# Segment sums of a graph kernel: gathered rows as the stationary operand, three tiles at a time

## The reference

```python
# part 1: two relational layers (8 relation types), then a layer norm
h = x
for l in range(2):
    W = einsum('rb,bio->rio', coeff[l], basis[l])
    msg = einsum('ni,rio->rno', h, W)[etype, src] * norm
    h = segment_sum(msg, dst, 2500) + bias[l]
    if l < 1: h = relu(h)
x = layernorm(x + h)
# part 2: three mean-aggregation layers, then a layer norm
h = x @ W_in + b_in
for l in range(3):
    agg = segment_sum(h[src], dst, 2500) / max(degree, 1)
    h = relu(agg @ W_agg[l] + h @ W_self[l] + b_hid[l])
out = layernorm(x + h @ W_out + b_out)
```

## Time and profile before

| | us |
|---|---|
| median of 3 runs (2393.61 to 2397.88) | 2394.03 |
| the profiled execution, its own time | 2401.69 |
| its span in the profile | 2399.9 |
| PE busy, matmuls | 1803.5 (75%) |
| POOL busy | 1255.5 (52%) |
| DVE busy | 1197.4 (50%) |
| ACT busy | 625.7 (26%) |

### The profile page before, as it was taken

The page is one execution under the profiler, slowest core; times in us unless marked ns, Lnnn a source line. Parts: engine busy times, 40 slices in busy tenths (PEclk is TensorE's granted clock), DMA queues, the critical chain, the costliest instruction groups (busy, mean ns, idle before and its releaser), DMA issues.

```text
span 2399.9 us, 29813 instructions
## 1 busy us (share of the span) xinstructions
PE 1803.5 (75%) x7695; PEld 1342.2 (56%) x7695; DVE 1197.4 (50%) x3965; ACT 625.7 (26%) x1520; POOL 1255.5 (52%) x1294
## 2 busy tenths in 40 slices
PE   4667677677677676757677777776666679999997
PEld 2455455455455454535455555555555567777776
DVE  5747654544445445335555555553268743232355
ACT  1112222222222222212222322222111124633332
POOL 5766666666666666366666666666666630000000
PEclk9879888988889899879989888899888789999998
DMA  6333333333333333233333333334533320000011
GB/s 209 93 89 97 99 98 98 100 97 98 99 99 97 99 99 99 59 92 101 102 100 98 105 99 100 103 101 122 169 102 96 98 61 11 1 1 1 1 35 44
DMA packets 118622, 208.19 MB, mean 87 GB/s; under 512 B 53828, under 2 KB 74196, under 8 KB 118456
## 3 DMA queue, kind: packets, MB, share of 16 engines
q0 software_dynamic: 62016, 169.04, 24.8%
q1 hardware_dynamic: 48848, 26.08, 3.8%
q10 hardware_dynamic: 7592, 11.13, 1.4%
HBM read 189.01 MB, written 17.13 MB: 86 GB/s over the span
## 4 chain that ended last, share of the span: by engine, by line
PE 50%; another core or an unknown queue 17%; issue 14%; DVE 13%; ACT 3%; DVEq 2%; DMA 1%; ACTq 0%; POOL 0%
PE bank L662 15%; PE bank L828 11%; PE bank L615 8%; DVE RY L455 4%; PE bank L650 4%; DVE RY L444 2%; PE bank L593 2%; PE bank L845 2%; PE bank L773 2%; DVE RY L379 1%; DVE RY L378 1%; DMA RX<-in_basis 1%; ACT RY L560 1%; DVE rdeg L390 1%
## 5 line engine op out<-in xcount | busy, mean ns | idle before, releaser
L662 PE MATMUL bank<-RY 128*128 128x256 f32 x2580 | 864.3, 432 | 11.6 <-issue 4.6
L250 POOL DMA_INDIRECT RY<-H,si x645 | 619.4, 960 | 367.0 <-issue 152.4
L250 POOL DMA_INDIRECT RY<-in_x,si x645 | 635.8, 986 | 333.1 <-issue 147.5
L444 DVE TENSOR_TENSOR RY<-RY,bank 128x256 f32 x430 | 180.8, 420 | 900.7 <-remote 694.8
L662 PEld LDWEIGHTS bank<-RY 128*128 128x128 f32 x2580 | 487.1, 220 | 109.4 <-issue 42.0
L650 PE MATMUL bank<-idn,RY 128*128 128x128 f32 x860 | 193.4, 311 | 394.7 <-issue 245.9
L455 DVE TENSOR_SCALAR RY<-iot,c,wgt 128x128 f32<-128x128 f32 x1290 | 461.8, 370 | 1.5 <-issue 1.5
L560 ACT COPY RY<-bank 128x256 f32<-128x256 f32 x430 | 161.1, 375 | 973.2 <-PE bank L662 519.8
L650 PEld LDWEIGHTS bank<-idn,RY 128*128 128x128 f32 x860 | 116.5, 158 | 503.4 <-issue 451.0
L828 PE MATMUL bank<-Ar,hs 125*128 125x500 f32 x1200 | 305.8, 405 | 0.0
L828 PEld LDWEIGHTS bank<-Ar,hs 125*128 125x128 f32 x1200 | 225.7, 188 | 51.7 <-issue 9.2
(11 more groups left out here) (106 smaller groups left out, 1163.2 us busy)
## 6 DMA issues: line engine op xcount, KB each, us to landing
RY<-in_x,si POOLq DMA_INDIRECT x645
RY<-H,si POOLq DMA_INDIRECT x645
Ad<-RY SPq DMA_DIRECT2D x215, 40.0 KB
RX<-Ad ACTq DMA_DIRECT2D x20, 305.2 KB
RX<-in_basis ACTq DMA_DIRECT2D x2, 2048.0 KB, 34.3
H<-RY SPq DMA_DIRECT2D x22, 128.0 KB
RY<-in_x SPq DMA_DIRECT2D x22, 128.0 KB
X<-RY SPq DMA_DIRECT2D x22, 128.0 KB
```

What stands on the lines that cost most here:

```text
L250: e.indirect_dma_start(G[0:k, n % NG, :], None, table, bass.IndirectOffsetOnAxis(ap=si[0:k, t:t + 1], axis=0)).then_inc(s_land[n % NG], 16)
L444: e.tensor_tensor(o, o, bank[4 + wg % 2][:, 0:256].rearrange("p (q c) -> p q c", c=16), ALU.add).then_inc(s_za, 1)
L662: e.matmul(bank[2 + wg % 2][:, 0:256], S[0:k, n % NSL, :], G[0:k, n % NG, :], start=(i == 0), stop=(i == TA - 1)).then_inc(s_sum, 1)
```

## The change

The sums are produced with features on the partitions at once. For each group, at its last tile, PE issues six matmuls: for each half of the features (c = 0, 1) and each of the three tiles, the half of the gathered rows `G` (128x128) is the stationary operand and `S` (128x128) the moving one. Both halves of a group lie in one bank, and the groups take banks 2 to 5 in turn. DVE adds that bank to `ZA` directly. The copy to `Zs`, the transposes and their semaphores are gone. `s_sum` still counts tiles, now each at its matmul for c = 1, the last reader of its slots. The waits elsewhere that named the removed semaphores name `s_sum`, `s_za` or `s_win`; the region `RY` is laid out without `Zs`.

```diff
@@ -172,9 +172,9 @@
 
         with ExitStack() as inner:
             RY = inner.enter_context(nc.sbuf_tensor("RY", [128, 20480], F32))
-        (Mr, Nr, Aw, Aw8, E2, G, S, Zs, W2, ZA, Ew, Pg, hw, h1w, xw, xT) = lay(
+        (Mr, Nr, Aw, Aw8, E2, G, S, W2, ZA, Ew, Pg, hw, h1w, xw, xT) = lay(
             RY, ((NSL, 128), BF16), ((NSL, NB), BF16), ((4, NB), BF16), ((4, NB), U8), ((2, 128), BF16), ((NG, 256), F32),
-            ((NSL, 128), F32), ((2, 256), F32), ((2, 2048), F32), ((2, 16 * ZC), F32), ((2, 128), F32), ((2, 256), F32),
+            ((NSL, 128), F32), ((2, 2048), F32), ((2, 16 * ZC), F32), ((2, 128), F32), ((2, 256), F32),
             ((2, 256), F32), ((2, 256), F32), ((2, 256), F32), ((2, 256), F32))
         ZA = ZA.rearrange("p s (q c) -> p s q c", c=ZC)
         diag = [v[:, k, h * 128:(h + 1) * 128] for v in (xw, xT) for k in range(2) for h in range(2)]
@@ -198,7 +198,7 @@
         s_land = [sem(f"s_land{i}") for i in range(NG)]
         s_sel, s_sum = sem("s_sel"), sem("s_sum")
 
-        s_zs, s_turn, s_za = sem("s_zs"), sem("s_turn"), sem("s_za")
+        s_za = sem("s_za")
 
         s_clear, s_carry1, s_prod, s_pg = sem("s_clear"), sem("s_carry1"), sem("s_prod"), sem("s_pg")
         s_hw, s_h1w, s_h1 = sem("s_hw"), sem("s_h1w"), sem("s_h1")
@@ -440,8 +440,8 @@
                 e.wait_ge(s_clear, 4 * (l * NW + g + 1))
             else:
                 e.wait_ge(s_za, wg)
-            e.wait_ge(s_turn, wg + 1)
-            e.tensor_tensor(o, o, bank[4 + wg % 2][:, 0:256].rearrange("p (q c) -> p q c", c=16), ALU.add).then_inc(s_za, 1)
+            e.wait_ge(s_sum, l * T + min(T, TA * w + TA))
+            e.tensor_tensor(o, o, bank[2 + wg % 4][:, 0:256].rearrange("p (q c) -> p q c", c=16), ALU.add).then_inc(s_za, 1)
 
         def dve_layer(e, l):
             for t in range(T + (TAIL if l == 0 else 2)):
@@ -552,12 +552,6 @@
                         act_clear(e, l, 0, k)
                 if t % TW in (24, 25, 26, 27) and t // TW + 1 < NW and t < T:
                     act_clear(e, l, t // TW + 1, t % TW - 24)
-                if t % TA == TA - 1 and t < T:
-                    wg = l * NA + t // TA
-                    if wg > 1:
-                        e.wait_ge(s_turn, wg - 1)
-                    e.wait_ge(s_sum, n + 1)
-                    e.copy(Zs[:, wg % 2, :], bank[2 + wg % 2][:, 0:256]).then_inc(s_zs, 1)
                 for g, k in STEPS[l].get(t, []):
                     act_post(e, l, g, k)
                 if l == 0 and t < 8 * WPE:
@@ -639,35 +633,34 @@
                                       xT[:, s, c * 128:(c + 1) * 128], start=(c == 0), stop=(c == 1))
                 mm.then_inc(s_win, 1)
 
-        def pe_turn(e, l, w):
-            wg = l * NA + w
-            if wg > 1:
-                e.wait_ge(s_za, wg - 1)
-            else:
-                e.wait_ge(s_idn, 1)
-            e.wait_ge(s_zs, wg + 1)
+        def pe_sums_of(e, l, t):
+
+            wg = l * NA + t // TA
+            if t % TA < TA - 1:
+                return
+            if wg > 3:
+                e.wait_ge(s_za, wg - 3)
+            e.wait_ge(s_sel, l * T + t + 1)
             for c in range(2):
-                mm = e.transpose(bank[4 + wg % 2][:, c * 128:(c + 1) * 128], Zs[:, wg % 2, c * 128:(c + 1) * 128], idn[:, :])
-            mm.then_inc(s_turn, 1)
+                for i in range(TA):
+                    n, k = l * T + t - TA + 1 + i, edge_rows(t - TA + 1 + i)
+                    if c == 0:
+                        e.wait_ge(s_land[n % NG], 16 * (n // NG + 1))
+                    mm = e.matmul(bank[2 + wg % 4][:, c * 128:(c + 1) * 128], G[0:k, n % NG, c * 128:(c + 1) * 128],
+                                  S[0:k, n % NSL, :], start=(i == 0), stop=(i == TA - 1))
+                    if c == 1:
+                        mm.then_inc(s_sum, 1)
 
         def pe_layer(e, l):
             for t in range(T + (TAIL if l == 0 else 2)):
                 n = l * T + t
                 if t < T:
-                    i, wg, k = t % TA, l * NA + t // TA, edge_rows(t)
-                    if i == 0 and wg > 1:
-                        e.wait_ge(s_zs, wg - 1)
-                    e.wait_ge(s_sel, n + 1)
-                    e.wait_ge(s_land[n % NG], 16 * (n // NG + 1))
-                    e.matmul(bank[2 + wg % 2][:, 0:256], S[0:k, n % NSL, :], G[0:k, n % NG, :], start=(i == 0),
-                             stop=(i == TA - 1)).then_inc(s_sum, 1)
+                    pe_sums_of(e, l, t)
                 for g, k in STEPS[l].get(t, []):
                     if k < 8:
                         pe_apply(e, l, g, k)
                     elif l == 1:
                         pe_post(e, g, k)
-                if t >= 4 and t % TA == 1 and t - 2 < T:
-                    pe_turn(e, l, (t - 4) // TA)
                 if l == 0 and t < 8 * WPE:
                     pe_weight(e, t)
                 if t < T:
@@ -818,7 +811,7 @@
                     e.wait_ge(s_pg, 2 * NW)
                     e.wait_ge(s_put, 2 * (NW - 1))
                 elif i == 1:
-                    e.wait_ge(s_zs, 2 * NA)
+                    e.wait_ge(s_za, 2 * NA)
                 else:
                     e.wait_ge(s_mean, 2 * (i - 1))
             e.wait_ge(*converted(n))
@@ -874,7 +867,7 @@
         def sp_load_x1(e, j):
             if j == 0:
                 e.wait_ge(s_x1d, 16 * NW)
-                e.wait_ge(s_x1t, NW)
+                e.wait_ge(s_win, NW)
             if j >= 4:
                 e.wait_ge(s_y, j - 3)
             e.dma_start(x1b[0:PB, j % 4, :], X1[j * PB:(j + 1) * PB, :]).then_inc(s_x1b[j % 4], 16)
@@ -962,7 +955,7 @@
 
         def act_mean_layers(e):
             last = NW - 1
-            e.wait_ge(s_turn, 2 * NA)
+            e.wait_ge(s_sum, 2 * T)
             e.wait_ge(s_ad, 16 * NA)
             e.wait_ge(s_A, 16 * JB)
             for n in range(NR):
```

## The result

The kernel after the change takes 2401.67 us (median of 15 runs, 2398.8 to 2403.89), the kernel before 2396.96 us beside it (15 runs): ratio 1.002, 95% interval 1.0013 to 1.0026. Forecast was 2304 us, with a range of 2180 to 2396 us. Nothing was gained; 4.7 us, 0.2%, were lost.

The account below looks back on a forecast made before the run. Part 1 was taken to wait rather than work, POOL losing 265 us to pauses for PE's late-seen sums. Longer runs (-88 us) and layer ends (-2 us) gave 2312 us from the profiled 2401.69, 2304 against the median; range 2180 to 2396 us.

Parts of the forecast that it names:

- step 1: PE's sums: twelve passes of 0.111 us per group replace sums and transposes, 98 us less PE time, counted as nothing.
- rival 4: PE's sums: weight loads don't hide, each pass waits for a load as long as itself; 2642 us, chance 0.03.
- Step 2: ACT: 430 copies of 0.375 us, 161 us, go; nothing for the time.
- steps 3 and 4: Waits for copy, sums and turn go, the addition waits for s_sum alone; next late is S, allowing nine tiles.
- Step 7: End of each layer: only the addition remains between last sum and first product, -1 us per layer, -2 us.
- step 5: POOL's pauses in both layers: nine tiles per pause instead of six shrink 265 us to 6/9, -88 us.
- rival 3: PE's wait for S of a group's third tile: whole groups shorten runs to five tiles, +53 us, 2447 us; chance 0.15.
- Step 4: Slots of S: one bunch of signals allows six tiles for certain and nine if luckily timed, before three and six.
- Rival 2: The S ring takes the turn's place, the beat stays six tiles; only 2 us gained, 2392 us, chance 0.12.
- Rival 1: Signals no longer late or no longer matter, POOL's 1.25 us per tile is the bound; 2127 us, chance 0.12.

Follow-up runs that it names:

- e_workplus2: Changed kernel with two more 128-column products per group into unused columns, repeated beside the kernel before at 2375.73 us: 2388.77 us, ratio 1.0058.
- e_rows32: Changed kernel with gathers of 32 rows instead of 128 after the first sixteen: 2377.04 us beside 2371.77 us for the kernel before.
- e_freegather: Changed kernel with gathers after the first sixteen sent to three spare slots nobody reads, PE multiplying stale rows: 3299.24 us beside 2371.77 us for the kernel before.
- e_s12: Changed kernel with 12 slots of S instead of 8: 2374.95 us, ratio 1.0003 to the kernel before.
- e_workplus: Changed kernel with two more 128-column products per group into unused columns: 2102.83 us beside 2109.48 us for the kernel before, ratio 0.997.
- e_halfgathers2: Changed kernel with only every second gather issued, odd tiles using stale rows, repeated beside the kernel before at 2375.73 us: 1691.52 us.
- e_halfgathers: Changed kernel with only every second gather issued, odd tiles using stale rows: 1676.98 us beside 2109.48 us for the kernel before.

## Why the prediction was wrong

**What held.** The bottleneck's place: POOL pauses because PE's sums come late, and not for lack of PE time. The size of the loss: 265 us of pauses by the prediction, and the same chip gives 2375.73 - 2109.48 = 266 us between the long and the short condition. The passes cost what step 1 said, 0.112 us for 0.111, with loads hidden (rival 4 is out), although PE's busy time fell by 32 us and not 98; I counted none of it, and e_workplus2 bears that out. Step 2 held (ACT's busy time fell by 145 us of the 161), and steps 3 and 4 named rightly which wait goes (L444) and which comes (`S`, L455). Step 7's 2 us are below what the runs tell.

**What failed is step 5**, "Nine tiles per pause: (9 x 1.25 + 1.43) / 9 = 1.41 us per tile". I had read pauses after six gathers only, and took their 1.43 us for a constant that a longer run spreads over more tiles. It isn't one. After nine gathers it is 13.18 - 9 x 1.25 = 1.93 us; after six of 1.17 us it is 8.85 - 7.02 = 1.83 (e_rows32). The mean is what stays, 1.46 to 1.49 us per gather in the long condition, across a beat of six or nine, rings of 8 and 12, of 8 and 16 slots, half the bytes, a quarter of the rows, one to six signals per group, and 2141 to 3887 passes in 800 us. The pause is the remainder of a rate that something else sets.

A run of six with its pause can't tell the one from the other, but the trace of the kernel before had runs of other lengths, which I noted under rival 3 ("it mixes shorter and longer beats") and did not measure. Here is one of nine gathers in it:

```profile
1042.35 0.95 POOL L250 DMA_INDIRECT RY<-H,si  x1 [1.95 <-PE bank L662]
...
1052.48 0.96 POOL L250 DMA_INDIRECT RY<-H,si  x1 [0.30 <-issue]
1055.55 0.95 POOL L250 DMA_INDIRECT RY<-H,si  x1 [2.11 <-PE bank L662]
```

It takes 13.20 us, where step 5 gives 9 x 1.25 + 1.43 = 12.68. Take every step over 1.45 us as the end of a run. Over both layers of that trace a pause then adds 0.9 us to a run of four or five gathers, 1.3 to one of six, 1.5 to one of seven or eight, and 1.7 to one of nine to eleven; single gathers lose 0.9 us each. So the pause was no constant before the change either. It grows less than in proportion in these rows, and by them alone step 5 would have promised less, not nothing; that the whole stays at one rate is what the kernel after and the experiments add.

The reading under step 5 was too narrow as well: "PE's completions are seen late while gathers are in flight". In e_freegather it is PE's own instructions that come one in 1.40 us: late signals are not all that holds PE while POOL issues.

**Step 4** failed in part: six tiles stayed the rule while counts ran (12 of 185 runs had nine or more), and nine became the rule only after them. By e_s12 it didn't matter.

**The rivals.** Rival 2 was nearest in time (2392 us, 0.12) for a wrong reason: not the ring of `S`, since with 12 slots nothing changes. Rival 1, POOL's pace, is what the short condition shows, but for the kernel before too (2109.48 us), so the change isn't what brings it. Rival 3 and its 53 us did not come. I had no rival for a rate that belongs to the gathers themselves; my last sentence looked for "late signals of another cause than gathers in flight", where the cause was the gathers, only not as a beat that can be stretched for a gain.

**What stays open.** What holds POOL's gathers and PE's instructions to about 1.47 us per gather, why the same program meets it at one time and not at another, and whether plain transfers escape it. No run separates a cause inside the core from one outside the program, such as the other cores or the recording itself; the "unknown queue" of the chain isn't identified. e_freegather fits with one thing that both need, which is always occupied when gathers come faster than 1.4 us or so; that is argued, not shown.

## What to carry to other kernels

When an engine's pauses come in a beat, compare beats of different length before pricing one: if the mean per item is the same, the pause is a remainder, and removing waits around it can move idle time from line to line without giving any back. Here 900 us of idle time left one line and 774 us appeared before another, for a gain of nothing. Before improving a chain of waits, take the suspected resource away altogether (here: no gathers, then every second one); two such runs said more than the edits of the chain. And run the kernel before beside every experiment: here its own time differed by an eighth on one chip (2109.48 and 2375.73 us).

## What was not expected of the hardware

- In the long condition POOL issuing indirect transfers without a pause brings PE to one instruction in 1.40 us, with nothing in the program between the two (e_freegather, one run: 526 PE instructions and 516 gathers in 700 us, clock 0.50). In the short condition it doesn't (e_workplus: 3459 passes beside 470 gathers in 590 us, clock 0.96). In the long one, at one gather in 1.77 us, a gather costs PE next to nothing (e_halfgathers2: 0.89 us per tile against 0.86).
- The same kernel takes 2109 or 2376 us on the same chip at two times, with gathers at 1.25 or 1.47 us. For kernels with all their gathers the page tells which: in the short condition it gives 2.8 us for a gather's landing and the chain has no unknown queue; in the long one the landing time is missing, and 12 to 28% of the chain is unknown (39% in e_freegather). With every second gather the two pages are nearly alike (e_halfgathers, e_halfgathers2: at most 1% unknown).
- A gather of a quarter of the rows saves POOL 0.08 us (1.25 to 1.17), so its price to POOL is nearly all fixed. Half as many gathers took the kernel to 1691.52 us, a quarter of the rows left it at 2377.04: fewer, not smaller, gathers are what would help.
